# A hand-written order for the end of the attention half of an attention and expert kernel

## The chip, the cores and the metric

One core of a Trainium2 chip runs the whole program. The time is device microseconds (us) of one execution; of several executions the median is given. Engines are named as the profile names them: PE (TensorE; PEld its weight loads), DVE (VectorE), ACT (ScalarE), POOL (GpSimd), SP (SyncE, which here only issues DMAs).

## What is computed

For 32 batches of 256 tokens with 512 features:

```
x = x + attention(layernorm(x), ctx)        # 16 heads of 32, one mask for all batches
xn2 = layernorm(x)
scores = softmax(xn2 @ w_gate)               # 8 experts; the two best are taken
place = running count of tokens per expert   # cumulative over all tokens, capacity 2048
x = x + sum over 2 of weight * expert(xn2)   # silu(a) * g, then a projection
```

The place of a token in its expert's list depends on all tokens before it, so batches are routed in order.

## The kernel before

The program has two blocks, each with one instruction stream per engine. `attention_block` does attention, the second normalisation and the routing; it writes x2 (x after attention) to `out`, xn2 to `xn2_rows`, and for every token two records (token and weight) to `table`. `expert_block` loads `table`, gathers the rows of xn2 by it and runs the experts. The second block begins when every engine has left the first, and POOL leaves last: it waits until all records have landed (line 417).

A batch is two tiles of 128 tokens and four chunks of four heads. Every engine runs `step(n)` for n from -2 to 34 (`STEPS`, line 236), and in a step works on up to four batches: the projections of batch n+1, the scores and softmax of batch n ("heads"), the end of batch n-1 ("tail": the output product, x2, the second normalisation) and the routing of batch n-2 ("late"). The order within a step is written out by hand on each engine and each engine's queue is in order, so a wait holds up all that stands behind it. Where a batch does not exist its part of the step falls away; steps 32, 33 and 34 hold only what the last batches have left.

The pieces that the change and the prediction touch:

- `scale(g)` (POOL, line 379): multiplies one head's probabilities by the inverse row sum that `invert(g)` (DVE, line 659) makes. Two instructions a head.
- `move(g)` (SP, line 262): 16 DMAs that turn the blocks of an even chunk; `attend(g)` (PE, line 940) of an even chunk waits for them. An odd chunk is turned on PE by `probs_turn` (line 901) and copied by ACT, `turned_out` (line 462).
- `attn_hi` (ACT, line 469) and `attn_lo` (DVE, line 628) split the attention output into two parts; `outputs(b, t, half)` (PE, line 1012) multiplies them by the output weights, six 512-column matrix products per call, into bank_b for tile 0 and bank_c for tile 1.
- `x2_out` (DVE, line 675), `moments_x2` (line 684: two BN_STATS and two BN_AGGR), `root(1, b, ...)` (POOL, line 343: two small operations that make 1/sqrt), `normalise_x2` (DVE, line 609).
- `x2_turn(b, t)` (PE, line 890) transposes xn2, `x2t_out` (ACT, line 436) copies it to `x2t`, which is the memory of `x2`; `gate`, `gate_out`'s copy (line 529), `gate_sum`, `logits_out` (DVE, line 691), `route` (line 697), `places` (PE, line 1044), `place_out` (line 726), `record` (line 736), and `records` (POOL, line 332: four indirect DMAs a batch). All of the routing's matrix products and both transposes share one PSUM bank, `bank_a`, so that the second transpose of a batch waits for the copy of the first.
- `add_bias` (POOL, line 367) forms x plus the output bias; `x2_store` and `xn2_store` stand for the DMAs of lines 559 and 505.

What POOL's last steps look like before:

```
if c == 3 and has(n):
    add_bias(n)
...
if c == 3 and has(n - 1):
    root(1, n - 1, ln2_var, ln2_chain, ln2_rstd, xn2_ready)
if has(n):
    for r in range(2 if c == 3 else 3, HPC):
        scale(g + r)
```

In step 31 this puts the second normalisation's root of batch 30 between the scales of the last four heads. On PE, step 32 begins with `probs_turn(127, 0)`, `x2_turn(30, 0)`, `probs_turn(127, 1)`, `x2_turn(30, 1)`, and the two other turns; then `gate(30)`, `attend(126)`, `attend(127)`, `gate_sum(30)` and the four calls of `outputs(31, ...)`. Chunks are counted through all batches, so 124 to 127 are those of batch 31.

Of the kernel before, what the change touches and what calls it, by code (L numbers as in the profile page):

```python
# [25 lines left out]
P = 128  # L26
# [45 lines left out]
def attention_block(nc, x, ctx_t, mask, w_attn, b_qk, b_v, b_o, w_gate, out, xn2_rows, table):  # L72
# [4 lines left out]
    with ExitStack() as stack:  # L77
# [58 lines left out]

        w_raw = [a.rearrange("p a t (c i) -> p (a t c) i", i=i).rearrange("p (c j) i -> p c (j i)", j=D // i)
# [29 lines left out]
        bank_c = ps("bank_c", [P, 512])  # L167

# [67 lines left out]
        STEPS = range(-2, BATCH + 3)  # L236

        def has(n):

            return 0 <= n < BATCH  # L240

# [13 lines left out]
        with nc.Block() as block:  # L255
# [45 lines left out]
            def _(pool):  # L301
# [85 lines left out]

                def step(n):
                    if n == -2:
                        root(0, 0, ln1_var, ln1_chain, ln1_rstd, xn_ready)  # L390
                    for c in range(DC):
# [9 lines left out]
                        if c == 3 and has(n):  # L401
                            add_bias(n)
# [5 lines left out]
                        if c == 3 and has(n - 1):  # L408
                            root(1, n - 1, ln2_var, ln2_chain, ln2_rstd, xn2_ready)
# [3 lines left out]

                for n in STEPS:
                    step(n)
                for i in range(2):
# [3 lines left out]
            def _(act):  # L420
# [15 lines left out]
                def x2t_out(b, t):  # L436
                    if t == 0:
                        act.wait_ge(x2_stored, b * 16 + 16)
                    act.wait_ge(x2t_full, b * TILES + t + 1)
                    nc.scalar.copy(x2t[:, :, t * P:(t + 1) * P], bank_a[:, :].rearrange(  # L440
                        "p (c i) -> p c i", c=DC)).then_inc(x2t_ready, 1)

# [46 lines left out]
                def step(n):  # L489
# [12 lines left out]
                    if late:  # L502
                        act.wait_ge(xn2_ready, n - 1)
                        settle(act)
                        act.dma_start(xn2_out[n - 2], xn2).then_inc(xn2_stored, 16)
# [20 lines left out]
                    if late:  # L526
                        act.wait_ge(gate_full, n - 1)
                        need(act, logits_full, n - 2)
                        nc.scalar.copy(gate_parts[:, :], bank_a[:, 0:SEQ]).then_inc(gate_copied, 1)
# [26 lines left out]
                    if tail:  # L556
                        act.wait_ge(x2_ready, n * TILES)
                        settle(act)
                        act.dma_start(out_rows[n - 1], x2).then_inc(x2_stored, 16)
# [5 lines left out]
                    if late:  # L565
                        act.wait_ge(fall_ready, n - 1)
                        nc.scalar.activation(weight_exp[:, :, :], fall[:, :, :], ACT.Exp).then_inc(weight_exped, 1)
# [10 lines left out]

                for n in STEPS:
                    step(n)  # L580

            @block.vector
            def _(dve):
# [107 lines left out]
                def logits_out(b):  # L691
                    dve.wait_ge(logits_full, b + 1)
                    need(dve, route_step, b * ROUTE)
                    nc.vector.tensor_copy(logits[:, :, :], bank_a[:, 0:TILES * EXPERTS].rearrange(
# [852 lines left out]
```

## Time and profile before

| | |
|---|---|
| median of 3 runs | 2895.09 us (2892.3 to 2896.34) |
| the profiled execution | 2895.05 us |
| its span, first to last instruction | 2893.3 us |
| attention half | up to 1288.18 us of the span |
| expert half | the rest |
| PE busy over the span | 97% |
| POOL busy over the span | 44% |

Times of instructions are counted from the start of the span. A row of the instruction view gives the start, the time to the end of the last instruction merged in it, the engine, the line of the kernel, the operation, what it writes and reads, and in brackets how long the engine had been idle and what ended that. Two rows can overlap, since an engine starts an instruction before the one ahead has ended. The tensors x2, xn2 and x2t are one buffer and appear as x_xn.

### The profile page before, as it was taken

How to read it: one execution, taken by the hardware profiler on the slowest of the kernel's cores; microseconds unless marked ns; L12 is line 12 of the kernel's file. 1: busy time of each engine (PE TensorE's matmuls, PEld its weight loads, DVE VectorE, ACT ScalarE, POOL GpSimd, SP SyncE). 2: the span in 40 equal slices, each digit the busy share in tenths (PEclk: the TensorE clock that was granted, in tenths of full speed). 3: DMA queues.
4: the chain of work that ended last, by engine and by line, in shares of the span. 5: the costliest groups of instructions: out<-in, count | busy, mean ns of one | idle time of the engine just before them, and what ended most of it. 6: DMA issues, size and time to landing. Idle time of an engine off the chain costs nothing.

```text
span 2893.3 us, 53420 instructions
## 1 busy us (share of the span) xinstructions
PE 2802.7 (97%) x17712; PEld 2299.0 (79%) x17712; DVE 1559.5 (54%) x5032; ACT 1400.8 (48%) x3688; POOL 1265.5 (44%) x1918
## 2 busy tenths in 40 slices
PE   6999999999999999949999999999999999999997
PEld 5888888888888888737888888888888888888886
DVE  6788888888888888843333242333332422423331
ACT  5777777777777777733233242232332322323221
POOL 5677777777777777652121212222222212121211
PEclk9999999999999999969999999999999999999999
DMA  4354444444334444335343434444443434344312
GB/s 145 100 113 112 110 118 111 114 114 118 101 106 114 108 118 115 92 91 145 84 92 88 84 95 81 99 84 91 89 94 81 102 79 104 77 89 92 71 30 29
DMA packets 214728, 280.59 MB, mean 97 GB/s; under 512 B 38464, under 2 KB 126528, under 8 KB 212928
## 3 DMA queue, kind: packets, MB, share of 16 engines
q1 hardware_dynamic: 151392, 143.84, 19.2%
q0 software_dynamic: 32768, 67.26, 13.5%
q10 hardware_dynamic: 30304, 66.07, 6.8%
q8 instruction: 153, 2.51, 0.4%
q14 instruction: 111, 0.91, 0.1%
HBM read 109.53 MB, written 67.90 MB: 61 GB/s over the span
## 4 chain that ended last, share of the span: by engine, by line
PE 53%; DMA 1%; issue 0%; ACT 0%; POOL 0%; DVE 0%; SPq 0%; POOLq 0%
PE a_ps L1481 18%; PE g_ps L1481 18%; PE y_ps L1496 18%; DMA fc_raw<-in_c_fc 1%; DMA out<-y,recs 1%; DMA xg<-xn_rows,lists 0%; POOL xg L1274 0%; DMA lists<-table 0%; ACT fc_hi L1337 0%; POOL out L1322 0%; ACT L1377 0%; ACT y L1393 0%; DVE hidden L1444 0%; ACT act_part L1377 0%; SPq L1216 0%
## 5 line engine op out<-in xcount | busy, mean ns | idle before, releaser
L1322 POOL DMA_INDIRECT out<-y,recs x128 | 205.2, 1603 | 1189.0 <-ACT y L1393 854.5
L384 POOL TENSOR_SCALAR probs<-probs,row_inv 128x256 f32<-128x256 f32 x1024 | 499.1, 502 | 270.6 <-DVE row_inv L662 264.3
L1444 DVE TENSOR_TENSOR hidden<-act_part,g_ps 128x512 f32<-128x512 f32 x192 | 132.1, 688 | 894.1 <-ACT act_part L1377 894.1
L484 ACT ACTIVATE probs<-probs,low 128x256 f32<-128x256 f32 x1024 | 511.2, 502 | 186.3 <-DVE low L653 161.8
L653 DVE CUSTOM_DVE_ANT_0 probs<-scores_ps,mask_add,row_any 128x256 f32<-128x256 f32 x1024 | 429.4, 474 | 29.1 <-PE scores_ps L971 28.2
L1481 PE MATMUL a_ps<-xe_hi,fc_hi 128*128 128x512 f32 x768 | 300.4, 391 | 4.1 <-DVE xe_lo L1400 2.6
L1496 PE MATMUL y_ps<-pj_hi,ht_hi 128*128 128x512 f32 x768 | 299.5, 390 | 0.7
L1481 PE MATMUL a_ps<-xe_lo,fc_hi 128*128 128x512 f32 x768 | 299.7, 390 | 0.0
L1481 PE MATMUL a_ps<-xe_hi,fc_lo 128*128 128x512 f32 x768 | 299.7, 390 | 0.0
L1481 PE MATMUL g_ps<-xe_hi,fc_hi 128*128 128x512 f32 x768 | 299.0, 389 | 0.0
L1496 PE MATMUL y_ps<-pj_hi,ht_lo 128*128 128x512 f32 x768 | 298.9, 389 | 0.0
L1481 PE MATMUL g_ps<-xe_lo,fc_hi 128*128 128x512 f32 x768 | 298.8, 389 | 0.0
L1496 PE MATMUL y_ps<-pj_lo,ht_hi 128*128 128x512 f32 x768 | 298.8, 389 | 0.0
L1481 PE MATMUL g_ps<-xe_hi,fc_lo 128*128 128x512 f32 x768 | 298.7, 389 | 0.0
L1377 ACT ACTIVATE act_part<-a_ps 128x512 f32<-128x512 f32 x192 | 115.0, 599 | 356.3 <-PE g_ps L1481 353.4
L1393 ACT ACTIVATE y<-y_ps,recs 128x512 f32<-128x512 f32 x128 | 88.2, 689 | 352.0 <-PE y_ps L1496 321.4
L1400 DVE TENSOR_TENSOR ht_lo<-hidden,ht_hi 128x512 fp32r<-128x512 f32 x192 | 133.0, 693 | 133.7 <-ACT ht_hi L1382 133.7
L1349 ACT CAST xe_hi<-x_turned 128x512 fp32r<-128x512 f32 x124 | 77.0, 621 | 242.7 <-DVE x_turned L1412 242.7
L484 ACT ACTIVATION_READ_ACCUMULATOR probs<-probs,low 128x1 f32 x1024 | 194.4, 190 | 0.0
L1382 ACT CAST ht_hi<-hidden 128x512 fp32r<-128x512 f32 x192 | 119.3, 621 | 146.7 <-DVE hidden L1444 146.7
L672 DVE STREAM_TRANSPOSE blocks<-probs 128x512 f32<-128x512 f32 x256 | 159.4, 680 | 30.7 <-POOL probs L384 30.7
L1481 PEld LDWEIGHTS a_ps<-xe_hi,fc_hi 128*128 128x128 f32 x768 | 144.7, 188 | 36.2 <-issue 3.2
(179 smaller groups left out, 6519.2 us busy)
## 6 DMA issues: line engine op xcount, KB each, us to landing
probs_m<-blocks SPq DMA_DIRECT2D x1024, 64.0 KB
x_quarters<-xg SPq DMA_DIRECT2D x496, 64.0 KB
fc_raw<-in_c_fc SPq DMA_DIRECT2D x24, 1024.0 KB, 5.8
out<-x_xn ACTq DMA_DIRECT2D x32, 512.0 KB, 2.8
xn_rows<-x_xn ACTq DMA_DIRECT2D x32, 512.0 KB, 5.1
cin<-in_ctx_t ACTq DMA_DIRECT2D x31, 512.0 KB, 6.0
xin<-in_x ACTq DMA_DIRECT2D x31, 512.0 KB, 4.4
pj_raw<-in_c_proj SPq DMA_DIRECT2D x8, 1536.0 KB, 6.6
```

Of the source, the lines that this page charges most:

```text
L384: last = nc.gpsimd.tensor_scalar(probs[:, r, t, :], probs[:, r, t, :], row_inv[:, r, t:t + 1], 1.0, ALU.mult, ALU.mult)
L484: last = nc.scalar.activation(probs[:, r, t, :], probs[:, r, t, :], ACT.Exp, scale=-1.0, bias=low[:, r, t:t + 1], accum_out=row_sum[:, r, ...
L653: last = nc.vector.tensor_tensor_reduce(out=probs[:, r, t, :], in0=scores_ps[g % HPC][:, t, :], in1=mask_add[:, t, :], scale=row_any[:, t: ...
L672: nc.vector.transpose(blocks[:, a, :].rearrange("p (b l) -> p b l", l=DK), of[:, :, a, :]).then_inc(turned, 1)
L1322: nc.gpsimd.indirect_dma_start(out=out[:, :], out_offset=bass.IndirectOffsetOnAxis(ap=recs[:, i * CT + t, 0:1].bitcast(U32), axis=0), in_= ...
L1377: nc.scalar.activation(act_part[:, m % 2, :], a_ps[m % 2][:, :], ACT.Silu).then_inc(silu_done, 1)
L1382: nc.scalar.copy(ht[0][:, m, :], hidden[:, m % 2, :]).then_inc(ht_hi_done, 1)
L1393: nc.scalar.activation(y[:, t, :], y_ps[t % 2][:, :], ACT.Copy, scale=recs[:, i * CT + t, 1:2].bitcast(F32)).then_inc(y_ready, 1)
L1400: nc.vector.tensor_tensor(dst, source, hi.bitcast(F32), ALU.subtract).then_inc(done, 1)
L1444: nc.vector.tensor_tensor(hidden[:, m % 2, :], act_part[:, m % 2, :], g_ps[m % 2][:, :], ALU.mult).then_inc(gated, 1)
L1481: last = nc.tensor.matmul(bank[:, :], fc[a][:, c * 2 + half, m * P:(m + 1) * P], xt[b][:, i % 2, c, :], start=first, stop=(c == DC - 1 and ...
L1496: last = nc.tensor.matmul(y_ps[t % 2][:, :], ht[a][:, m, t * P:(t + 1) * P], pj[b][:, m, :], start=first, stop=(m == MC - 1 and (a, b) == ...
```

## The change

The loop ends with step 31. Behind it each engine runs a `drain()` of its own. Step 31 itself changes in three places: POOL drops `add_bias(31)` and the root of batch 30 from it, and DVE puts `attn_lo` of chunks 124 and 125 behind the last two inversions. In the drain all four `probs_turn` come first, half of batch 31's output product goes ahead of `attend(126)`, and batch 30's transposes and gate are spread behind. Batch 31's x2, moments, root and normalisation are done tile by tile. The transposes of batch 31 go to two PSUM banks (`scores_ps[0]`, `[1]`), its gate and its places to two others, and the copies `x2t` of batches 30 and 31 go to unused parts of `probs` in place of the memory of x2. In the diff the four `drain()` stand in the order POOL, ACT, DVE, PE.

```
-        STEPS = range(-2, BATCH + 3)
+        STEPS = range(-2, BATCH)
+        LAST = BATCH - 1
...
+        def turned_of(b):
+            return x2t if b < LAST - 1 else x2t_last[b - LAST + 1]
+        def gate_bank(b):
+            return bank_a if b < LAST else last_banks[2]
+        def place_bank(b):
+            return bank_a if b < LAST else last_banks[3]
+        def x2_bank(b, t):
+            return bank_a if b < LAST else last_banks[t]
...
+                def last_root(t):
+                    pool.wait_ge(ln2_var, BATCH + t)
+                    pool.wait_ge(xn2_ready, LAST)
+                    settle(pool)
+                    nc.gpsimd.tensor_scalar(shifted[:, 1, t:t + 1], moments[:, 1, t, 1:2], LN_EPS, 0.0,
+                                            ALU.add, ALU.add).then_inc(ln2_chain, 1)
+                    pool.wait_ge(ln2_chain, BATCH + t)
+                    nc.gpsimd.tensor_tensor(rstd[:, 1, t:t + 1], shifted[:, 1, t:t + 1], half_pow[:, t:t + 1],
+                                            ALU.pow).then_inc(ln2_rstd, 1)
+                def drain():
+                    root(1, LAST - 1, ln2_var, ln2_chain, ln2_rstd, xn2_ready)
+                    add_bias(LAST)
+                    for i in range(TILES * TOP_K):
+                        records(LAST - 2, i)
+                    for t in range(TILES):
+                        last_root(t)
+                    for b in (LAST - 1, LAST):
+                        for i in range(TILES * TOP_K):
+                            records(b, i)
...
-                        if c == 3 and has(n):
+                        if c == 3 and has(n) and n < LAST:
                             add_bias(n)
...
-                        if c == 3 and has(n - 1):
+                        if c == 3 and has(n - 1) and n < LAST:
                             root(1, n - 1, ln2_var, ln2_chain, ln2_rstd, xn2_ready)
...
                 def x2t_out(b, t):
                     if t == 0:
-                        act.wait_ge(x2_stored, b * 16 + 16)
+                        if b < LAST - 1:
+                            act.wait_ge(x2_stored, b * 16 + 16)
+                        else:
+                            act.wait_ge(turned, BATCH * DC // 2 * GROUPS)
...
+                def drain():
+                    g = LAST * DC
+                    for r in range(HPC):
+                        turned_out(g + 3, r)
+                    xn2_store(LAST - 1)
+                    attn_hi(g + 2)
+                    attn_hi(g + 3)
+                    for t in range(TILES):
+                        x2t_out(LAST - 1, t)
+                    gate_out(LAST - 1)
+                    x2_store(LAST)
+                    x2t_out(LAST, 0)
+                    xn2_store(LAST)
+                    x2t_out(LAST, 1)
+                    fall_exponents(LAST - 1)
+                    gate_out(LAST)
+                    fall_exponents(LAST)
...
-                        need(dve, logits_full, b)
+                        if b < LAST:
+                            need(dve, logits_full, b)
+                        else:
+                            dve.wait_ge(logits_full, b - 1)
+                            dve.wait_ge(x2_stored, b * 16)
...
+                def drain():
+                    g = LAST * DC
+                    record(LAST - 2)
+                    attn_lo(g + 2)
+                    attn_lo(g + 3)
+                    for t in range(TILES):
+                        x2_out(LAST, t)
+                        dve.wait_ge(x2_ready, LAST * TILES + t + 1)
+                        settle(dve)
+                        last_moments(t)
+                    last_normalise(0)
+                    logits_out(LAST - 1)
+                    last_normalise(1)
+                    route(LAST - 1)
+                    place_out(LAST - 1)
+                    record(LAST - 1)
+                    logits_out(LAST)
+                    route(LAST)
+                    place_out(LAST)
+                    record(LAST)
...
                 def x2_turn(b, t):
-                    pe.wait_ge(xn2_ready, b + 1)
-                    if t:
+                    pe.wait_ge(xn2_ready, b + 1 + (t if b == LAST else 0))
+                    if b == LAST:
+                        pass
+                    elif t:
                         pe.wait_ge(x2t_ready, b * TILES + 1)
...
+                def drain():
+                    g = LAST * DC
+                    for r in range(HPC):
+                        probs_turn(g + 3, r)
+                    outputs(LAST, 0, 0)
+                    attend(g + 2)
+                    attend(g + 3)
+                    x2_turn(LAST - 1, 0)
+                    outputs(LAST, 1, 0)
+                    outputs(LAST, 0, 1)
+                    x2_turn(LAST - 1, 1)
+                    outputs(LAST, 1, 1)
+                    gate(LAST - 1)
+                    gate_sum(LAST - 1)
+                    x2_turn(LAST, 0)
+                    x2_turn(LAST, 1)
+                    places(LAST - 1)
+                    gate(LAST)
+                    gate_sum(LAST)
+                    places(LAST)
```

`last_moments(t)` is one BN_STATS and one BN_AGGR, `last_normalise(t)` one tensor_scalar of a tile; `gate_out`, `fall_exponents`, `x2_store` and `xn2_store` are the old lines of ACT's step as functions.

## Rows read from the trace of the kernel before

**Rows 1.** Chain that ended last, at the second block's start: start, us, what.

```profile
1288.18 2.47 DMA lists<-table
```

**Rows 2.** Instructions in order of time, POOL, 1246 to 1284 us.

```profile
1246.13 1.84 POOL L384 TENSOR_SCALAR probs<-probs,row_inv 128x256 f32<-128x256 f32 x4 [2.71 <-DVE row_inv L662]
...
1249.99 2.28 POOL L384 TENSOR_SCALAR probs<-probs,row_inv 128x256 f32<-128x256 f32 x4
...
1266.46 0.23 POOL L348 TENSOR_SCALAR shifted<-moments 128x2 f32<-128x2 f32 x1 [8.14 <-DVE moments L595]
...
1279.18 0.96 POOL L337 DMA_INDIRECT table<-rec,place_i  x1 [3.91 <-DVE place_i L764]
...
1283.00 0.97 POOL L337 DMA_INDIRECT table<-rec,place_i  x1 [0.30 <-issue]
```

**Rows 3.** Instructions in order of time, DVE, 1248 to 1279 us.

```profile
1248.60 0.84 DVE L631 SCALAR_TENSOR_TENSOR at_lo<-attn_ps,bias_v,at_hi 128x256 fp32r<-128x256 f32 x2
...
1263.83 0.69 DVE L681 TENSOR_TENSOR x_xn<-bank_c,x_bo 128x512 f32<-128x512 f32 x1 [0.79 <-PE bank_c L933]
1264.63 1.29 DVE L591 BATCH_NORM_STATS2 stats<-x_xn 128x6 f32<-128x512 f32 x2
1266.02 0.25 DVE L595 BATCH_NORM_AGGREGATE moments<-stats 128x2 f32<-128x6 f32 x2
...
1267.52 1.00 DVE L600 TENSOR_SCALAR x_xn<-x_xn,moments,rstd 128x512 f32<-128x512 f32 x2 [1.12 <-POOL rstd L351]
...
1274.91 0.17 DVE L694 COPY logits<-bank_a 128x16 f32<-128x16 f32 x1 [5.03 <-PE bank_a L1039]
1275.21 0.24 DVE L703 MAX8 top<-logits 128x8 f32<-128x8 f32 x2
...
1278.19 0.17 DVE L764 CAST place_i<-place_f 128x4 int32<-128x4 f32 x1
```

**Rows 4.** Instructions in order of time, PE, 1231 to 1274 us.

```profile
1231.39 0.63 PE L933 MATMUL bank_b<-w_lo,at_hi 128*128 128x512 f32 x1
1231.82 0.63 PE L933 MATMUL bank_b<-w_hi,at_lo 128*128 128x512 f32 x1
...
1251.08 1.12 PE L876 MATMUL bank_a<-ident,x_xn 128*128 128x128 f32 x4 [3.31 <-DVE x_xn L600]
1251.99 1.06 PE L909 MATMUL scores_ps<-ident,probs 128*128 128x128 f32 x4
...
1256.49 1.05 PE L954 MATMUL attn_ps<-probs_t,v 128*32 128x256 f32 x16
...
1263.17 0.40 PE L933 MATMUL bank_c<-w_lo,at_hi 128*128 128x512 f32 x1
1263.40 0.39 PE L933 MATMUL bank_c<-w_hi,at_lo 128*128 128x512 f32 x1
...
1268.58 1.11 PE L876 MATMUL bank_a<-ident,x_xn 128*128 128x128 f32 x4 [4.67 <-DVE x_xn L600]
...
1272.28 1.08 PE L1030 MATMUL bank_a<-x_xn,wg 128*32 128x256 f32 x8 [0.67 <-ACT x_xn L440]
```

**Rows 5.** Instructions in order of time, ACT (ACTq: its DMAs), 1257 to 1270 us.

```profile
1257.61 0.84 ACT L477 ACTIVATE at_hi<-attn_ps,bias_v 128x256 fp32r<-128x256 f32 x2 [1.36 <-PE attn_ps L954]
...
1268.61 0.37 ACTq L505 DMA_DIRECT2D xn_rows<-x_xn  x1
1269.79 0.58 ACT L440 COPY x_xn<-bank_a 128x512 f32<-128x512 f32 x1 [4.54 <-PE bank_a L876]
```

**Rows 6.** Instructions in order of time, SP: the DMAs of chunk 126's move.

```profile
1241.73 10.24 SPq L270 DMA_DIRECT2D probs_m<-blocks  x16
```

**Rows 7.** Stretches: length, busy us of PE, PEld, DVE, ACT, POOL, granted clock, DMA share, GB/s.

```profile
1252.00:1254.00 2.00, 2.00 (x10) 1.66 (x10) 0.76 (x6) 1.17 (x2) 0.87 (x2) 0.50 0.94 320
1254.00:1256.00 2.00, 2.00 (x25) 1.55 (x27) 0.00 (x0) 1.74 (x4) 1.45 (x2) 0.87 0.04 9
```

**Rows 8.** One line's instructions, whole run: ns least, median, most.

```profile
L337 POOL DMA_INDIRECT table<-rec,place_i x128: 964/976/1237, 153.8 to 1283.0; - x128
```

More of the change, by code:

```diff
@@ L167, in attention_block @@
         bank_c = ps("bank_c", [P, 512])
+        last_banks = [scores_ps[r][:, :, :].rearrange("p t k -> p (t k)") for r in range(HPC)]
         setup_loaded = sem("setup_loaded")
@@ L415, in _ @@
                     step(n)
+                drain()
                 for i in range(2):
@@ L437, in x2t_out, with xn2_store, x2_store, gate_out @@
                     if t == 0:
-                        act.wait_ge(x2_stored, b * 16 + 16)
+                        if b < LAST - 1:
+                            act.wait_ge(x2_stored, b * 16 + 16)
+                        else:
+                            act.wait_ge(turned, BATCH * DC // 2 * GROUPS)
                     act.wait_ge(x2t_full, b * TILES + t + 1)
-                    nc.scalar.copy(x2t[:, :, t * P:(t + 1) * P], bank_a[:, :].rearrange(
+                    nc.scalar.copy(turned_of(b)[:, :, t * P:(t + 1) * P], x2_bank(b, t)[:, :].rearrange(
                         "p (c i) -> p c i", c=DC)).then_inc(x2t_ready, 1)
+                def xn2_store(b):
+                    act.wait_ge(xn2_ready, b + (1 if b < LAST else TILES))
+                    settle(act)
+                    act.dma_start(xn2_out[b], xn2).then_inc(xn2_stored, 16)
+                def x2_store(b):
+                    act.wait_ge(x2_ready, (b + 1) * TILES)
+                    settle(act)
+                    act.dma_start(out_rows[b], x2).then_inc(x2_stored, 16)
+                def gate_out(b):
+                    act.wait_ge(gate_full, b + 1)
+                    need(act, logits_full, b)
+                    nc.scalar.copy(gate_parts[:, :], gate_bank(b)[:, 0:SEQ]).then_inc(gate_copied, 1)
+                def fall_exponents(b):
+                    act.wait_ge(fall_ready, b + 1)
+                    nc.scalar.activation(weight_exp[:, :, :], fall[:, :, :], ACT.Exp).then_inc(weight_exped, 1)
                 def qk_out(which, b, half, bank):
@@ L502, in step @@
                     if late:
-                        act.wait_ge(xn2_ready, n - 1)
-                        settle(act)
-                        act.dma_start(xn2_out[n - 2], xn2).then_inc(xn2_stored, 16)
+                        xn2_store(n - 2)
                     if heads:
@@ L526, in step @@
                     if late:
-                        act.wait_ge(gate_full, n - 1)
-                        need(act, logits_full, n - 2)
-                        nc.scalar.copy(gate_parts[:, :], bank_a[:, 0:SEQ]).then_inc(gate_copied, 1)
+                        gate_out(n - 2)
                     if tail:
@@ L565, in step @@
                     if late:
-                        act.wait_ge(fall_ready, n - 1)
-                        nc.scalar.activation(weight_exp[:, :, :], fall[:, :, :], ACT.Exp).then_inc(weight_exped, 1)
+                        fall_exponents(n - 2)
                     if heads:
@@ L853, in step @@
                         moments_x2(n - 1)
-                    if heads:
+                    if heads and n < LAST:
                         attn_lo(g)
                         attn_lo(g + 1)
+                    if heads:
                         invert(g * HPC + 3 * HPC + 2)
@@ L861, in step @@
                         invert(g * HPC + 3 * HPC + 3)
+                    if n == LAST:
+                        attn_lo(g)
+                        attn_lo(g + 1)
                     if tail:
```

38 lines of the change are left out of this document (26 added, 12 removed).

## The prediction

> **What bounds the kernel now.** I read the chain that ended last first. In order of time its first transfer is the load of `table` at 1288.18 us [rows 1], the first act of the expert half. Nothing in the diff touches that half, so I take it as a block that starts when the attention half ends. All the change can do is to move this moment.
>
> So I followed the attention half's end backwards through the instructions in order of time. The last work before 1288.18 is POOL's fourth indirect DMA of batch 31's records, at 1283.00; from there to 1288.18 lie 5.18 us of landing and leaving the block, which the change does not touch. The four DMAs start 1.27 us apart ((1283.00 - 1279.18) / 3), and the first 0.82 us after `place_i` (1278.19 + 0.17 = 1278.36) [rows 2, 3]. Before that nothing overlaps: normalisation of both tiles (ends 1267.52 + 1.00 = 1268.52, call this moment T), two transposes each with a copy between, gate, sum, logits at 1274.91, routing, `place_i` [rows 3, 4, 5]. That is 14.48 us from T to the last record's start. Before T stand the x2 of tile 1 at 1263.83, two BN_STATS, the aggregates and POOL's root [rows 2, 3]. And before 1263.83 PE multiplies the last output product, which it could only begin after the attention of the last two chunks (from 1256.49) [rows 4]. In this last stretch the granted clock matters: PE idled for want of work, the clock stood at 0.50 (1.2 GHz) from 1252 to 1254 and came back to 2.4 GHz within the next stretch; from its mean of 0.87 the rise was at 1254 + 2 x 0.26 = 1254.5 [rows 7]. That is 3.4 us after PE got steady work at 1251.08 [rows 4].
>
> **The change, part by part.** I count three terms against the profiled execution.
>
> Term 1, from step 31 to the x2 of tile 1. Before, POOL did the root of batch 30 between the last four heads' scales, and scaled the last two heads from 1249.99 to 1252.27 (four instructions in 2.28 us beside DVE's normalisation; four took 1.84 us without it) [rows 2]. Now the inversions come where `attn_lo` stood, at 1248.60 [rows 3], so I put these scales at 1248.94 to 1250.78. PE turns the last two heads from about 1249.92 and 1250.83; at the low clock one turn takes 0.91 us (1251.08 to 1251.99) [rows 4], so PE is free at 1251.75. It then does half of tile 0's output product, six at the low clock, where one takes 0.43 us (1231.39 to 1231.82): to 1254.4. Then `attend(126)` and `attend(127)`, at the high clock 0.86 us apart: I take the second from 1255.3 to 1256.36, against 1256.49 + 1.05 = 1257.54 before [rows 4]. The move of chunk 126 does not hold it: its last DMA is issued by 1241.73 + 10.24 = 1251.97 and the DMA engines are quiet soon after 1254 [rows 6, 7].
>
> After the attention, ACT and DVE need 0.84 us and 0.88 us for the last two splits [rows 3, 5], so the parts are whole at 1258.2. PE does not wait for them: it has batch 30's first transpose (0.44 us) and half of tile 1, six at 0.23 us (1263.17 to 1263.40) [rows 4], to 1258.0; the second half of tile 0, with the second split just in time, to 1259.4; the second transpose to 1259.85; the last six to 1261.27, and their result 0.16 us later. x2 of tile 1 starts at 1261.47 in place of 1263.83: **2.36 us**. Tile 0's x2, moments and root lie beside the last six products.
>
> Moved steps on the other queues. ACT now has the store of batch 30's xn2 ahead of the last two `attn_hi`. The root of batch 30 comes after the scales (1250.8 to 1251.9) and its normalisation ends at about 1253.0, 3.4 us before ACT could begin `attn_hi`; cost nothing. POOL's `add_bias` (2.6 us) and `records(29)` (four at 1.27) follow that root and end near 1260.4; the first `last_root` can start at 1261.1. Cost nothing, but with 0.7 us of cover only; beyond that, 1 us more is free because the first tile's normalisation stands behind the second tile's moments anyway. SP's queue keeps its order. The wait for the store of batch 30's x2 is for a DMA issued 20 us earlier.
>
> Term 2, from there to T. Before: 1268.52 - 1263.83 = 4.69 us. Now one tile's statistics and not two (1.29 / 2 saved), one aggregate, and one tile's normalisation behind the root (0.5 saved) [rows 3]. From row to row: x2 at 1261.47, BN_STATS at 1262.27, aggregate 1263.03 to 1263.2, root to 1264.41 (as 1266.46 to 1267.52 before) [rows 2, 3], normalisation to T' = 1264.95. That is 3.48 us: **1.21 us** saved.
>
> Term 3, from T to the last record. Batch 30's routing was done before T; now it comes behind it, and so do batch 30's four records. DVE routes at once: from MAX8 to the end of `place_i` 3.15 us (1275.21 to 1278.36) [rows 3]; the copies and transposes of batch 31 run beside it. POOL starts the first of eight records at T' + 3.10 + 0.82 = T' + 3.92, the last 7 x 1.273 later: T' + 12.83. Batch 31's own chain needs less: gate at T' + 1.9 (PE turns both tiles without waiting for a copy, one turn and its copy taking 1.79 us from 1268.58 to 1270.37 [rows 4, 5]), logits 2.63 us later (1272.28 to 1274.91), `place_i` 3.45 later, T' + 7.98, so its first record could go at T' + 8.8 where POOL is free at T' + 9.0. POOL's issue of records is what ends last, by a hair. 14.48 - 12.83 = **1.65 us**.
>
> Sum: 2.36 + 1.21 + 1.65 = 5.2 us. 2895.05 - 5.2 = 2889.85 for the profiled execution; the median of the runs stands 0.04 us above it, so 2889.9.
>
> Bounds of what no row shows. The second half of the drain's clock: if PE got the high clock as soon as it has steady work, term 1 gains at most 1.0 us more (the move's landing near 1253.5 stops it); if the rise comes 2 us later, it loses 1.0 us, because PE works at half rate. The price of leaving the block: that wait and its 5.18 us stay, and I see no reason for a gain or loss over 0.5 us. The records in a row of eight: 1.27 us apart, or at worst each longer by 1237 - 976 = 261 ns [rows 8], 2.1 us for eight.
>
> Against the last there is a row and a rule. The scales beside the normalisation took 2.28 us and not 1.84 [rows 2]. "SBUF — State Buffer" of the Trainium skill, section "SBUF: two separate sides", says that VectorE and GpSimd share a port pair as an exclusive lock, and that GpSimd cannot write the descriptors of its DMAs while VectorE holds it. By that rule batch 30's records, which now run beside batch 31's routing on DVE, would be slowed, which makes the rival C below.
>
> **The rivals.** Over and under 0.2% (5.8 us) is what a measurement of this kernel can tell from no change.
>
> A, the sum as it stands: 2889.9, a gain of 5.2 us, within 0.2%. Chance 0.52.
>
> B, PE comes to the high clock earlier, or it does not fall as deep, since it now gets turns at 1247, 1248 and 1250 without a hole of 3.3 us: 1.0 us more, and with smaller cover than I gave to the small steps 2888.7. Faster by over 0.2%. For it: the work is denser. Against: the clock had fallen with these same first turns under way. Chance 0.34.
>
> C, POOL's queue grows: eight records in a row beside DVE's routing at up to 0.26 us more each, or `records(29)` holding up the first root past its 1.7 us. It gives 2.1 us back: 2892.0. Against: most records of the whole run sit beside a busy DVE and their median is 976 ns [rows 8]. Chance 0.08.
>
> D, slower: PE never gets back the high clock in the drain, since from 1254.5 on it goes from one short group to the next. Place: all from `attend(126)` to the last output product. Price: 18 products at 0.20 us (3.6), two attentions (1.7), two transposes (0.9): 6.2 us against 5.2, so 2896.0. It decides when the clock stays low to beyond 1264.7 (5.2 us lost at half rate from 1254.5 on), where my count has the product finished at 1261.3. Against: PE has less than 0.1 us of holes there by my count, and before it rose with holes of 0.2 us. "TensorE: Matmul & The Clock Gate" of the Trainium skill, section "A second HAM failure mode: psum-queue depth-cycling", tells of a kernel whose PE idled briefly between groups and whose clock went back and forth. Chance 0.03.
>
> E, the end is held by something else (a store landing, the block's end) and the change moves nothing: 2895.1. Against: the last store, of xn2, is issued at 1268.61 [rows 5], 14 us before POOL's last record. Chance 0.03.
>
> **How the numbers follow.** 2889.9 is case A. The range: downward to B and 2 us of spread between executions, 2886.8; upward it takes in C and the late clock with the same spread, 2893.8; D and E are left out. Faster by over 0.2% is B: 0.34; within it A, C and E, 0.62; slower D and half a point of E, 0.04.
>
> **What would show it.** In the changed profile: `lists<-table` at 1283.0; eight L337-type DMAs on POOL at 1.27 us without a hole, the first at 1268.9; x2 of tile 1 at 1261.5; the tile's normalisation ending at 1265.0; `attend(127)` at 1255.3; the clock back at 1254.5. A hole between the two batches of records would say that batch 31's chain and not POOL ends last. A POOL root of the first tile after 1262.9 would say that records hold it. The expert half must keep its length, 2893.3 - 1288.18 = 1605.1 us; if that changes by more than a microsecond the prediction is wrong for a reason that I don't have.

## The result, and the profile after

The changed kernel takes 2888.86 us (median of 12 runs, 2887.35 to 2892.58), the kernel before 2894.9 (12 runs, 2892.3 to 2896.34). The ratio is 0.9982, 95% interval [0.9974, 0.9989]: a gain of 3.2 to 7.5 us, 6.0 by the medians. Forecast were 2889.9 and 5.2 us. In run 1 below, one execution took 4016 us at a granted clock of 0.653; it is left out of the numbers there.

The profiled execution took 2888.59 us, its span is 2886.8: 6.50 us less than before. To see where they come from I measure from one **mark** in both traces, the start of the BN_STATS over batch 30, the last event on DVE before the two orders part. (POOL's `add_bias(31)` stood 6 us ahead of it in the kernel before and is gone there, but PE's attention of chunk 125, which begins before that addition, already starts 0.52 us sooner, at 1240.17 and not 1240.69.) DVE in order of time, the line of the kernel before, then those of the changed one:

```profile
1246.75 1.26 DVE L591 BATCH_NORM_STATS2 stats<-x_xn 128x6 f32<-128x512 f32 x2
```

```profile
1246.22 1.26 DVE L671 BATCH_NORM_STATS2 stats<-x_xn 128x6 f32<-128x512 f32 x2
...
1251.36 2.93 DVE L680 TENSOR_SCALAR x_xn<-x_xn,moments,rstd 128x512 f32<-128x512 f32 x2 [2.15 <-POOL rstd L373]
...
1261.03 0.69 DVE L765 TENSOR_TENSOR x_xn<-bank_c,x_bo 128x512 f32<-128x512 f32 x1
...
1263.99 0.55 DVE L965 TENSOR_SCALAR x_xn<-x_xn,moments,rstd 128x512 f32<-128x512 f32 x1 [0.69 <-POOL rstd L418]
...
1267.42 0.17 DVE L848 CAST place_i<-place_f 128x4 int32<-128x4 f32 x1
...
1272.29 0.17 DVE L848 CAST place_i<-place_f 128x4 int32<-128x4 f32 x1
```

x2 of tile 1 starts 14.81 us behind the mark; before it was 1263.83 - 1246.75 = 17.08 [rows 3]. **T**, the end of the last normalisation, is 1264.54, 3.51 us behind the start of x2 of tile 1 (4.69 before). POOL in order of time:

```profile
1248.37 1.84 POOL L406 TENSOR_SCALAR probs<-probs,row_inv 128x256 f32<-128x256 f32 x4 [0.93 <-DVE row_inv L742]
...
1251.31 2.70 POOL L398 TENSOR_TENSOR x_bo<-xin,bias_o 128x512 f32<-128x512 f32 x2
...
1260.11 0.97 POOL L359 DMA_INDIRECT table<-rec,place_i  x1 [0.30 <-issue]
1261.09 0.27 POOL L415 TENSOR_SCALAR shifted<-moments 128x1 f32<-128x1 f32 x1
...
1268.42 1.08 POOL L359 DMA_INDIRECT table<-rec,place_i  x1 [4.47 <-DVE place_i L848]
...
1277.44 0.97 POOL L359 DMA_INDIRECT table<-rec,place_i  x1 [0.30 <-issue]
```

The last two heads' scales are four in 1.84 us, where they took 2.28 beside DVE [rows 2]. The eight records stand without a hole, (1277.44 - 1268.42) / 7 = 1.29 us apart, and the last starts 12.90 us behind T (14.48 before). Then the chain that ended last, at the second block's start:

```profile
1283.09 2.42 DMA lists<-table
1289.60 3.71 DMA xg<-xn_rows,lists
1294.80 18.65 DMA pj_raw<-in_c_proj
```

From the last record to this load it is 5.65 us (5.18 before). The account:

| stretch | before | after | gained |
|---|---|---|---|
| start to the mark | 1246.75 | 1246.22 | 0.53 |
| mark to x2 of tile 1 (term 1) | 17.08 | 14.81 | 2.27 |
| to T (term 2) | 4.69 | 3.51 | 1.18 |
| to the last record (term 3) | 14.48 | 12.90 | 1.58 |
| to the load of the lists | 5.18 | 5.65 | -0.47 |
| expert half | 1605.12 | 1603.71 | 1.41 |

So 5.03 of the 6.50 us lie where the change was made; the rest is 0.53 us ahead of the mark and 1.41 in the expert half, less 0.47 in leaving the block. Below, **D** is the distance from the mark to the last record's start, 36.25 us before and 31.22 after: it has the three terms and nothing of what differs between executions before the mark or in the expert half. A second profile of the changed kernel (run 11) has 30.95, so that a difference in D of 0.3 us or less says nothing. The distance from T to the last record varies less: 12.88 to 12.93 us in the seven profiles that leave this stretch as it is in the changed kernel.

PE in order of time, and the stretches around the return of the clock:

```profile
1251.03 0.78 PE L1059 MATMUL bank_b<-w_hi,at_hi 128*128 128x512 f32 x1
...
1253.84 1.07 PE L1080 MATMUL attn_ps<-probs_m,v 128*32 128x256 f32 x16
1254.72 1.05 PE L1080 MATMUL attn_ps<-probs_t,v 128*32 128x256 f32 x16
...
1260.60 0.40 PE L1059 MATMUL bank_c<-w_hi,at_lo 128*128 128x512 f32 x1
...
1264.59 1.12 PE L999 MATMUL scores_ps<-ident,x_xn 128*128 128x128 f32 x4 [0.66 <-DVE x_xn L965]
```

```profile
1252.00:1254.00 2.00, 2.00 (x9) 1.15 (x11) 2.00 (x2) 0.00 (x0) 2.00 (x2) 0.56 0.17 41
1254.00:1256.00 2.00, 2.00 (x35) 1.08 (x28) 1.50 (x13) 0.16 (x1) 0.00 (x1) 1.00 0.38 139
1264.00:1266.00 2.00, 1.20 (x7) 0.80 (x8) 1.69 (x12) 0.85 (x2) 0.00 (x0) 0.50 0.29 107
```

The granted clock, third from the end of a row, has the mean 0.56 from 1252 to 1254: 0.50 (1.2 GHz), then 1.00 (2.4 GHz) for 0.12 of the stretch. That puts the rise at 1254 - 2 x 0.12 = 1253.8, 7.5 us behind the mark (before, 7.8). Up to the last output product PE has no hole. From 1264 on it works at 1.2 GHz.

### The profile page after: what moved, and what is told of

Read it like the earlier page. It is cut to its first block, busy times and chain, and to the rows that moved or that the text cites. A ratio compares the mean times of both kernels' runs of the same rounds, so it can differ in the third digit from the quotient of the medians.

```text
span 2886.8 us, 53422 instructions
## 1 busy us (share of the span) xinstructions
PE 2802.8 (97%) x17712; PEld 2297.5 (80%) x17712; DVE 1560.5 (54%) x5032; ACT 1401.0 (49%) x3688; POOL 1267.5 (44%) x1920
## 4 chain that ended last, share of the span: by engine, by line
PE 53%; DMA 1%; DVE 1%; issue 0%; ACT 0%; POOL 0%; SPq 0%; POOLq 0%
PE y_ps L1645 18%; PE a_ps L1630 18%; PE g_ps L1630 18%; DMA pj_raw<-in_c_proj 1%; DMA out<-y,recs 0%; DVE pj_lo L1549 0%; DMA xg<-xn_rows,lists 0%; DVE hidden L1593 0%; DVE ht_lo L1549 0%; ACT ht_hi L1531 0%; POOL xg L1423 0%; DVE x_turned L1561 0%; DMA lists<-table 0%; ACT act_part L1526 0%; DVE xe_lo L1549 0%
## 5 line engine op out<-in xcount | busy, mean ns | idle before, releaser
L752 DVE STREAM_TRANSPOSE blocks<-probs 128x512 f32<-128x512 f32 x256 | 159.4, 680 | 30.7 <-POOL probs L406 30.7
```

Of the source, the lines that this page charges most:

```text
L752: nc.vector.transpose(blocks[:, a, :].rearrange("p (b l) -> p b l", l=DK), of[:, :, a, :]).then_inc(turned, 1)
```

## The experiments

The theory: the three terms add up; PE's and POOL's order in step 31 make the first, one tile's chain instead of two the second, and the third ends with POOL's queue of eight records, not with batch 31's routing. Each run undoes one part, or takes away what a rival says bounds it. All are edits of the changed kernel. Each was run beside the kernel before; the ratios are to it, and comparisons by D come from one profile each. In the code, `...` marks what is left out.

**1. The last normalisation for both tiles at once.**

```diff
-    last_moments(t)
-last_normalise(0)
+moments_x2(LAST)
+normalise_x2(LAST)
 logits_out(LAST - 1)
-last_normalise(1)
...
-for t in range(TILES):
-    last_root(t)
+root(1, LAST, ln2_var, ln2_chain, ln2_rstd, xn2_ready)
```

> The drain as changed, but the last normalisation done for both tiles at once again (statistics, root, normalisation of batch 31). I measure D, from the start of batch 30's BN_STATS in step 31 to the start of the last record on POOL: 36.25 us before, 31.22 us changed. If doing it tile by tile is worth the 1.2 us of my term 2, D is 32.4 us and the kernel about 1.2 us slower than the changed one. Rival: the tile-wise form is hidden beside PE and POOL and gives nothing, D 31.2.

2891.08 us, ratio 0.9989 [0.9979, 0.9999]. x2 of tile 1 comes at mark + 14.87, and from there to T it is 4.69 us again, to the hundredth what it was before. D is 33.32, 2.10 more than in the changed kernel and not the 1.2 expected, since T to the last record grew too, by 0.86:

```profile
1266.39 1.97 PE L995 MATMUL scores_ps<-ident,x_xn 128*128 128x128 f32 x8 [3.11 <-DVE x_xn L679]
```

Both turns now run in a row at 1.2 GHz behind T, and batch 30's places wait behind them. Tile by tile the first turn is over before T. So undoing the tile-wise form costs 2.1 us, of which my term 2 had only the first part. Some of the 0.86 is the clock: in the changed kernel the first turn still ran at 2.4 GHz, in 0.66 us.

**2. One bank for the end: batch 31's turns, gate and places in `bank_a`, with the waits that this needs.**

```diff
-return bank_a if b < LAST else last_banks[t]
+return bank_a
...
+if t:
+    pe.wait_ge(x2t_ready, b * TILES + 1)
+else:
+    pe.wait_ge(logits_copied, b)
...
+pe.wait_ge(x2t_ready, BATCH * TILES)
 places(LAST - 1)
+pe.wait_ge(place_used, LAST)
```

> The drain as changed, but batch 31's transposes, gate and places go to bank_a again, with the waits that this needs. If the last stretch is set by POOL's eight records and by how soon batch 30's place is known, only the wait of places(30) for the second copy counts: D 31.6 to 31.7 us against 31.22. Rival: the separate banks are what shortened the last stretch from 14.48 to 12.90 us: D 32.8 or more.

2890.1 us, 0.9985 [0.9976, 0.9995]; D 32.19, 0.97 more; T to the last record 13.66 (+0.76). That is between the two expectations (31.6 to 31.7, or 32.8 and more).

```profile
1266.42 1.09 PE L999 MATMUL bank_a<-ident,x_xn 128*128 128x128 f32 x4 [0.82 <-ACT probs L489]
1268.19 0.19 PE L1184 MATMUL bank_a<-member,before 128*128 128x8 bf16 x1 [0.68 <-ACT probs L489]
```

The second turn waits for the copy of the first, and the places of batch 30 for the copy of the second. They hold up batch 30's `place_i`, the head of POOL's queue, so the delay reaches the end: this `place_i` ends 3.78 us behind T and not 3.05. The banks are a part of term 3; the other 0.21 us of D lie ahead of x2, where this run differs in nothing.

**3. POOL's step 31 as before: root between the scales, `add_bias` back in the step.**

```diff
-if c == 3 and has(n) and n < LAST:
+if c == 3 and has(n):
     add_bias(n)
...
-if c == 3 and has(n - 1) and n < LAST:
+if c == 3 and has(n - 1):
     root(1, n - 1, ln2_var, ln2_chain, ln2_rstd, xn2_ready)
```

> The drain as changed, but POOL does add_bias(31) and the root of batch 30 in step 31 again, the root between the last two pairs of heads. My term 1: the last scales end 1.4 to 1.5 us later, and D grows by 0.8 to 1.5 us (less where the PE clock has come back by then), to 32.0 to 32.7. Rival: PE's own order (half of the output product ahead of the attention) hides it, D 31.2.

2890.98 us, 0.9987 [0.9977, 0.9997]; x2 of tile 1 at mark + 15.81 (+1.00), D 32.20 (+0.98).

```profile
1248.93 2.27 POOL L406 TENSOR_SCALAR probs<-probs,row_inv 128x256 f32<-128x256 f32 x4
```

With the root ahead (0.23 + 0.72 us) and DVE's normalisation beside them the scales take 2.27 us again; against the mark they start 1.1 us and end 1.5 us later. So about 1.0 of term 1's 2.27 us is POOL's order. The other 1.3 are left for PE's order and for `attn_lo` behind the inversions; no run separates these two. The run also says what ends last. Here the clock stayed at 2.4 GHz for the last turns (granted 1.00 from 1264 to 1266, 0.50 in the changed kernel), and batch 31's `place_i` ended 7.16 us behind T in place of 7.92. The last record was still 12.88 us behind T: 0.76 us less on batch 31's chain brought nothing. POOL's queue of records is what ends last.

**4. `add_bias(31)` alone back in step 31.**

```diff
-if c == 3 and has(n) and n < LAST:
+if c == 3 and has(n):
     add_bias(n)
...
-add_bias(LAST)
```

> The changed kernel with add_bias(31) back in step 31, where POOL idles anyway; the root of batch 30 stays in the drain. In the changed kernel this addition (2.70 us) ran beside batch 30's normalisation, which took 2.93 us and not 1.09. My account: that is covered, the normalisation falls back to about 1.0 us and ends near mark + 6.2 us in place of 8.07, and D stays at 31.2 us (mark: the start of batch 30's BN_STATS). Rival: the normalisation held ACT's store and attn_hi, or PE's transpose, and D falls by 1 us or more.

2888.45 us, 0.9984 [0.9975, 0.9993]; D 31.29 against 31.22.

```profile
1250.76 1.00 DVE L679 TENSOR_SCALAR x_xn<-x_xn,moments,rstd 128x512 f32<-128x512 f32 x2 [2.15 <-POOL rstd L373]
```

Without the addition beside it the normalisation of batch 30 takes 1.00 us, not 2.93, and ends 1.93 us sooner (mark + 6.14, not 8.07). Nothing else moves: it is covered.

**5. Batch 30's four records left out** (their tokens never reach the table, so batch 30's part of the lists is missing; POOL's wait at the end is lowered to match).

```diff
-for b in (LAST - 1, LAST):
+for b in (LAST,):
```

> The changed kernel without the four record DMAs of batch 30 (their tokens keep the default record and get no expert output). If batch 31's own chain ends almost as late as POOL's queue of eight records, as I counted (0.2 to 0.4 us earlier), the last record starts 0.25 to 0.4 us earlier: D 30.8 to 31.0. Rival: POOL's issue of records alone is what ends last, and dropping four of eight at 1.27 us takes up to 5.1 us away: D 26 to 27.

2888.73 us, 0.9978 [0.9969, 0.9988]; D 31.11, T to the last record 12.69.

```profile
1274.80 1.07 POOL L359 DMA_INDIRECT table<-rec,place_i  x1 [9.35 <-DVE place_i L848]
...
1278.73 0.97 POOL L359 DMA_INDIRECT table<-rec,place_i  x1 [0.30 <-issue]
```

Four of eight DMAs are gone, and measured from T the last starts 0.21 us sooner. Batch 31's own chain stands that close ahead of the queue's end; up to the last record a shorter queue is worth no more.

**6. PE kept busy: 22 products of constants into `bank_c`, whose result nobody reads, in PE's holes of step 31 and between the first turns.**

```diff
+def warm(count):
+    for _ in range(count):
+        nc.tensor.matmul(bank_c[:, :], w_hi[:, 3, 0, 0:P], w_hi[:, 3, 1, :], start=True, stop=True)
...
+        pe.wait_ge(x2_ready, LAST * TILES)
+        warm(16)
...
 for r in range(HPC):
     probs_turn(g + 3, r)
+    warm((1, 5, 0, 0)[r])
```

> The changed kernel with 22 matrix products of constants into the free bank_c, where PE would idle at the end of step 31 and between the first turns, so that the granted clock should stay at 1.00. They compute nothing that is used. My account of term 1: the turns and the first six products run at 2.4 GHz, the attention starts when the move of chunk 126 has landed, and x2 of tile 1 comes 0.5 to 1.7 us earlier (mark + 13.1 to 14.3 in place of 14.81), D 29.5 to 30.7. Rival: the chain before the x2 of tile 1 is not PE's (POOL's scales, the move or ACT hold it), and D stays within 0.3 us of 31.2.

2886.24 us, 0.9976 [0.9967, 0.9985], the lowest of all. PE in order of time and one stretch:

```profile
1251.77 0.40 PE L1063 MATMUL bank_b<-w_hi,at_lo 128*128 128x512 f32 x1
1253.47 1.07 PE L1084 MATMUL attn_ps<-probs_m,v 128*32 128x256 f32 x16 [1.30 <-DMA probs_m<-blocks]
```

```profile
1250.00:1252.00 2.00, 1.89 (x10) 1.44 (x10) 0.79 (x1) 1.07 (x2) 1.83 (x4) 1.00 0.28 69
```

The granted clock stayed at 1.00 up to 1262, beyond the last output product, and the last of the first six products started at mark + 5.70 (1253.31 in the changed kernel, mark + 7.09). Then PE waited 1.30 us for the move of chunk 126 and began the attention at mark + 7.40, where the changed kernel does at mark + 7.62. D is 31.02, 0.20 less, and not 29.5 to 30.7: the rival of the expectation came true. That is within what two profiles of the changed kernel differ by, so a PE twice as fast in this stretch is worth 0.2 us at most; the move of chunk 126 stops it.

**7. The old order up to the x2 of batch 31, the new one from there.**

```diff
-for r in range(HPC):
-    probs_turn(g + 3, r)
-outputs(LAST, 0, 0)
+probs_turn(g + 3, 0)
+x2_turn(LAST - 1, 0)
+probs_turn(g + 3, 1)
+x2_turn(LAST - 1, 1)
+probs_turn(g + 3, 2)
+probs_turn(g + 3, 3)
+gate(LAST - 1)
 attend(g + 2)
 attend(g + 3)
...
+gate_sum(LAST - 1)
+outputs(LAST, 0, 0)
...
```

ACT, DVE and POOL have their old order there too.

> The old order on all engines up to the x2 of batch 31 (POOL's root between the heads, batch 30's transposes and gate ahead of the attention), but batch 31's tile-wise normalisation, its own banks and the order behind it as changed. If the terms add up: x2 of tile 1 at mark + 17.1 us as before, then 3.5 and 12.9 us as changed, D 33.5 (before 36.25, changed 31.22). Rival: the parts depend on each other, for instance POOL's records of batch 29 or batch 30's late routing, and D is off by more than 0.5 us.

2890.85 us, 0.999 [0.998, 0.9999]; D 34.70, where 33.5 was expected. T is 3.51 us behind x2 and the last record 12.92 behind T, as in the changed kernel: terms 2 and 3 do not hang on term 1. The first part missed: x2 of tile 1 at mark + 18.27, not 17.1.

```profile
1254.00:1256.00 2.00, 2.00 (x20) 0.98 (x22) 0.00 (x0) 1.28 (x3) 1.69 (x2) 0.50 0.04 5
1256.00:1258.00 2.00, 2.00 (x36) 1.11 (x28) 0.00 (x0) 0.46 (x2) 0.97 (x1) 1.00 0.02 1
```

PE was busy from 1250 on, yet the clock rose only near 1256, mark + 10.3 (before: mark + 7.8). That is 2.5 us more at half rate, or 1.2 us. The clock had also fallen sooner, at the mark and not 0.9 us behind it as before, so that it stood at 1.2 GHz for 10.2 us and not 6.8. With the same order up to x2, the kernel before and this run had the high clock back at different moments.

**8. Batch 30 routed early:** its turns ahead of the attention (the second into a bank of its own) and its routing on DVE ahead of the x2, with `add_bias` back and 32 constant products (22 as in run 6, 10 ahead of, between and behind the last turns and the gate).

```diff
+x2_turn(LAST - 1, 0)
+x2_turn(LAST - 1, 1)
 attend(g + 2)
 attend(g + 3)
...
+logits_out(LAST - 1)
+route(LAST - 1)
 for t in range(TILES):
     x2_out(LAST, t)
```

> A version that may beat both: add_bias(31) back in step 31, PE kept busy with constants in its holes, and batch 30 transposed before the attention and routed on DVE where it waited for the output product, so that its records start right behind the normalisation. If POOL's eight records end last by a hair in the changed kernel (e5: batch 31's chain alone 0.2 us earlier), this helps only as far as batch 31's own chain gets faster too: T to last record 11.8 to 12.6 us in place of 12.90, and x2 of tile 1 0.5 to 1.5 us earlier; D 29.0 to 30.4. Rival: the routing on DVE delays the x2 of tile 0 and 1 and eats the gain, D 31 or more.

D is 29.94 as expected, 1.28 less than in the changed kernel, and the load of the lists comes at 1281.44, 1.65 us sooner. But the run takes 2895.03 us, 1.0007 [0.9998, 1.0016]: the expert half grew to 1611.8 us. What PE waited for in the expert loop (line, releaser: us in total, times, longest), and one of the waits:

```profile
PE a_ps L1644 <- issue: 7.5, 6, 1.9
```

```profile
1693.38 0.40 PE L1644 MATMUL a_ps<-xe_hi,fc_lo 128*128 128x512 f32 x1 [1.11 <-issue]
```

These are six waits that no other engine ends; the changed kernel has none. Five of them, 1.1 to 1.9 us long and 198 us apart, stand ahead of the sixth product of a turn of the expert loop, one in each turn but the first, that is in every turn which PE enters by jumping back. The sixth is 0.16 us ahead of a turn's first product. Either the new order does this or PE's longer program ahead of the loop, which sets where the loop's instructions lie.

The next three runs were made for it, on a chip on which every kernel took some 70 us more (before: 2964.77), so only their parts are compared. A part of the 70 us is of the same kind: in the changed kernel (run 11) PE waits there for no other engine 27 times, 42.1 us in all, on the transposes into `bank_a` (line 999) of the attention half, and in its first profile never.

**9. Run 8 with 10 of the 32 products.**

```diff
-warm(16)
-warm((1, 5, 0, 0)[r])
```

> The early routing version without the 22 constant products of step 31 and the turns; the ten behind places(30) stay. From e6 the first 22 are worth 0.2 us at most, since chunk 126's move ends at mark + 7.4 us; so x2 of tile 1 at mark + 15.1 to 15.5 us and D 30.0 to 30.6 (e8 29.94). For the expert half: in e8 it took 1611.8 us against 1601.7 to 1606.2 in all others, with six waits of PE for its own instructions (7.5 us in total), one for each turn of the expert loop. If that comes from where the loop's code lies behind PE's longer program, it is gone here with 20 added instructions and not 64, and the half is 1602 to 1606 us. Rival: it comes from the new order (an earlier or denser start), and the half is 1610 us or more again.

2965.73 us, 0.9986 [0.9965, 1.0007]. Expert half 1604.4 us, no such waits: the order alone does not bring them. D missed: 33.02, and not 30.0 to 30.6. The granted clock was 0.50 until 1355, 8.5 us behind the mark, and ACT began `attn_hi` 3.1 us behind the start of the second attention (1.1 in run 8). The trace names no engine of this core that ended ACT's wait of 3.23 us; why it came is left open.

**10. Run 6 with 10 more products at PE's very end, 32 in all, the changed kernel's order.**

```diff
 places(LAST)
+pe.wait_ge(x2_ready, BATCH * TILES)
+warm(10)
```

> e6 with ten more constant products behind places(31), where PE idles until the experts: 32 in all, as in e8, with the changed order. D stays at 31.0 (they stand behind everything that counts). If the place of the loop's code is what slowed the expert half of e8, it is 1610 us or more here too, with six waits of PE for its own instructions. Rival (the new order of e8 did it): 1602 to 1606 us.

2969.03 us, 1.0003 [0.9979, 1.0026]; D 31.27, no less than in the changed kernel; expert half 1611.9 us.

```profile
PE a_ps L1640 <- issue: 6.5, 5, 1.6
```

All five stand ahead of the sixth product of a turn again, in the five turns behind the first. With 32 products (each a weight load and a matmul, 64 instructions) ahead of the loop the waits come, in runs 8 and 10, which differ in order and chip; with 22 or 10 they do not, in either order (runs 6, 9, 12). This is shown. Where the border lies, and what of the loop meets it, is open. By "Runtime: NRT & Kernel Launch" of the Trainium skill, section "Instruction fetch mechanics", a taken branch whose target is outside what is fetched ahead stalls the engine. The waits fit that in so far as only the turns entered by a jump have them. But they stand behind the turn's fifth product and not at its first, and no run here looks at the fetch itself.

**11. The changed kernel again, on this chip.**

> The changed kernel once more, beside the two others on the same chip: D 31.2 us, its three terms within 0.2 us of 2.27, 1.18 and 1.58, and an expert half between 1602 and 1606 us, which would show that its 1.4 us less in the first profile is the spread of that half and no work of the change.

2961.74 us, 0.9989 [0.9969, 1.0009]: on this chip, with its wider spread, the gain is not clear of nothing. Mark to x2 14.51 us, then 3.51, then 12.93, D 30.95, expert half 1604.2. So the last two distances repeat within 0.03 us and the first within 0.3, because the clock came back 6.8 us behind the mark and not 7.5. The kernel before was not profiled on this chip.

**12. Run 8 with 22 products.**

> The early routing version with 22 constant products in all (ten in step 31, five between the turns, seven in the last stretch), as many as in e6 and not 32 as in e8. If both findings hold, the drain is e8's (D 29.9 to 30.5 us against 31.2 changed and 36.25 before) and the expert half e6's (1602 to 1606 us, no wait of PE for its own instructions): about 1 us faster than the changed kernel, a ratio to the kernel before near 0.9978. Rival: ten products in step 31 don't hold the clock, x2 of tile 1 comes at mark + 17 us or later as in e10, and the version is slower than the changed kernel.

2888.1 us, 0.9981 [0.9972, 0.999]. Expert half 1602.4 us, no such waits. D is 30.90, 0.3 less than in the changed kernel and not the 0.7 to 1.3 expected:

```profile
1264.00:1266.00 2.00, 1.79 (x8) 1.33 (x9) 1.39 (x11) 0.59 (x1) 0.81 (x2) 0.67 0.52 197
```

With fewer products the clock fell near 1264.7, and those that were left then ran at 1.2 GHz ahead of the gate. Its ratio to the kernel before is the changed kernel's (0.9981 and 0.9982). No version here clearly beats the changed kernel; run 6 has the lowest ratio (0.9976), with an interval that overlaps the changed kernel's, and all but 0.2 us of its lead lies outside D.

## Why the prediction was right, and where not

The forecast (2889.9, case A) held: 2888.86, within 0.2% by its ratio, inside the range. The three terms came out at 5.03 us of the 5.2 forecast. That the whole came as near is in part luck. The median is in fact nearer to case B's 2888.7, but what B named did not bring it: the surplus is the 0.53 us ahead of the mark and the 1.41 in the expert half. And the load of the lists came at 1283.09, where I had written 1283.0, because those 0.53 us and the 0.47 more for leaving the block nearly cancel. Step by step:

**Term 1**, 2.36 forecast, 2.27 measured. The way was right: PE free at the turns' end, half of tile 0 at the low clock, `attend(127)` at 1254.72 (forecast 1255.3, or 1254.8 after moving it by the mark's 0.5 us). Run 3 takes 1.0 us of the term away. "The move of chunk 126 does not hold it" is true by 0.2 us only (run 6). I had written for case B that the move near 1253.5 stops a further gain at 1.0 us. It landed at mark + 7.40, which counted from the mark of the kernel before is 1254.15, and stops it at 0.2.

**Term 2**, 1.21 forecast, 1.18 measured, and 1.18 again when undone (run 1). But undoing the tile-wise form costs 2.1 in all: my term 3 had the gate at T' + 1.9 without saying that it needs both the first turn ahead of T (0.86, run 1) and the banks (0.76, run 2). The sum was right, its split between the parts of the diff was not. These 0.86 and 0.76 us are not to be added: each run undoes one condition of the same early gate.

**Term 3**, 1.65 forecast, 1.58 measured: first record at T + 3.88 (T' + 3.92), eight at 1.29 us. "POOL's issue of records is what ends last, by a hair" is true: by 0.21 us (run 5), and freeing 0.76 us of the other chain does nothing (run 3).

**The covers.** I gave the normalisation of batch 30 until 1253.0. It ended at 1254.29, because `add_bias` ran beside it: 2.93 us for two tiles, 1.00 alone (run 4). The 3.4 us of cover absorbed that. `records(29)` waited for a `place_i` that DVE could only make behind this normalisation; they ended at 1261.08 and not 1260.4, and the first root began at 1261.09, right behind them. Of the 0.7 us of cover for POOL nothing was left. Of the free microsecond behind it 0.6 were: the first root ended at 1262.02, and the first tile's normalisation, at 1262.66, directly follows the aggregate of the second.

**The rivals.** B did not happen: the clock came back 0.3 us sooner against the mark, and holding it up throughout gives 0.2 us at most (run 6), so its 1.0 us was mis-sized, and with it the reason for a chance of 0.34. C: the records kept their pace, 1.29 us. What the Trainium skill says of GpSimd's descriptors ("SBUF — State Buffer", section "SBUF: two separate sides") shows no effect here: the eight stand 1.29 us apart beside the small operations of the routing, 1.27 in the kernel before. D: the clock stood at 1.00 from 1254 to 1264 and fell only behind the output product. E: the load of the lists moved by 5.09 us.

**The expert half.** I wrote that a change there by more than a microsecond would come from a reason that I don't have, and it changed by 1.41. All but 0.02 of it arises within its first 70 us; from there PE keeps the same step in both. Counted from the load of the lists, PE's first product came 0.65 us sooner, and the first twelve products of the first expert took 4.45 us and not 5.28, since the clock was back at 2.4 GHz after 18.4 us and not after 21.0. The chain waits there for other loads: `pj_raw` after, `fc_raw` in the kernel before:

```profile
1299.19 14.59 DMA fc_raw<-in_c_fc
```

Over the profiles of the kernels without the loop's waits this half is between 1601.7 and 1606.2 us long, and the two shown lie inside, 1.4 apart; the changed kernel again has 1604.2 (run 11). So I read it as spread, for which the forecast had 2 us of range. That the earlier start has no part in it is not shown. The leaving of the block took 0.47 us more than before, just inside the 0.5 that I had allowed without a reason. It took 5.65 us here, and 4.95 to 5.3 in runs 1 to 4, 6, 7, 10 and 11, all with eight records in a row; with a pause ahead of the last four it was 5.18 in the kernel before and 4.5 to 4.65 in runs 8, 9 and 12. Four records alone took 4.59 (run 5). So perhaps some 0.5 us are given back to the longer row of records. The kernel before speaks against it, and it was not tested by itself.

## What to carry to other kernels

Where a stretch has no overlap left, sum it from the rows of the kernel before, event by event: three terms of 1 to 2 us each came out within 0.1 us. Then ask of every term how far behind it the next chain stands. Here two chains ended 0.2 us apart, twice, so that the obvious next steps (a high clock, half the records) were each worth 0.2 us at most. And compare a small change by the distance between two events on either side of it; the whole time moves by as much as the gain for reasons elsewhere.

## What the hardware showed that I had not expected

**A row of a profile can be long because of its neighbour.** DVE's normalisation in the changed kernel, and the addition on POOL beside it (ns least, median, most):

```profile
L680 DVE TENSOR_SCALAR x_xn<-x_xn,moments,rstd x2: 1501/1502/1504, 1251.4 to 1252.8; 128x512 f32<-128x512 f32 x2
```

```profile
L398 POOL TENSOR_TENSOR x_bo<-xin,bias_o x2: 1268/1364/1459, 1251.3 to 1252.5; 128x512 f32<-128x512 f32 x2
```

One tile takes 0.55 us without POOL (L965) and 1.50 beside it, while POOL's loses little. "SBUF — State Buffer" of the Trainium skill, section "SBUF: two separate sides", gives a reason, a port pair that goes to whichever began first. POOL began 0.05 us ahead, and the trace agrees in direction. It does so too in the kernel before, where DVE began its normalisation 0.06 us ahead of POOL's scales: there DVE's took 1.09 us for two tiles, near the 1.00 alone, and POOL's scales were the ones that lost (2.28 and not 1.84 us). I had cited this rule for the records, where it did nothing, and not for `add_bias`, where it made DVE's normalisation 1.9 us longer.

**The clock's return is not fixed by the work.** Where no constant products held the clock up ahead of the turns, it came back 6.8 to 8.5 us behind the mark in nine profiles and 10.3 in run 7, with nearly the same work. Two profiles of the changed kernel differ by 0.7 us in it (7.5 and 6.8). In run 7 it moved x2 by 1.2 us, as much as a term of the sum.

**Instructions that cost nothing where they stand can cost elsewhere.** Ten more constant products, beside 22 others, at PE's idle end of the attention half brought 6.5 us of waits to a loop that they have no part in (run 10; 7.5 in run 8), as much as the whole change had gained.
